# ScalarE copies the turned rows two decays earlier in a scan slot, and makes the two gates behind two decays

## The reference

```
def step(state, inp):                 # selective scan over L = 512 steps
    d, b, c, u = inp
    dA = jnp.exp(d[..., None] * A)
    state = state * dA + (d * u)[..., None] * b[:, None, :]
    y = jnp.einsum('bdn,bn->bd', state, c)
    return (state, y)
...
y = y + D[None, :, None] * x
y = y * silu(z)
...
x = x + scan_part
h = _layernorm(x)
gu_s = h @ shared_gate_up             # shared expert, 2 x 352 = 704 wide
y = routed_experts + _swiglu(gu_s, SI) @ shared_down
out = x + y
```

## Time and profile before

| | |
|---|---|
| time, median of 3 runs (lowest, highest) | 1090.23 us (1086.03, 1094.56) |
| the profiled execution | 1086.13 us, span 1084.4 us |
| busy PE | 911.1 us (84%) |
| busy DVE | 832.5 us (77%) |
| busy POOL | 752.9 us (69%) |
| busy ACT | 514.5 us (47%) |
| granted TensorE clock, mean | 0.908 |

### The profile page before, as it was taken

The page is one execution under the profiler, slowest core; times in us unless marked ns, Lnnn a source line. Parts: engine busy times, 40 slices in busy tenths (PEclk is TensorE's granted clock), DMA queues, the critical chain, the costliest instruction groups (busy, mean ns, idle before and its releaser), DMA issues.

```text
span 1084.4 us, 16598 instructions
## 1 busy us (share of the span) xinstructions
PE 911.1 (84%) x4352; PEld 672.4 (62%) x4353; DVE 832.5 (77%) x1349; ACT 514.5 (47%) x959; POOL 752.9 (69%) x482
## 2 busy tenths in 40 slices
PE   4876656678899888879988899969999899998993
PEld 1322334455566666656656555639999799987992
DVE  4787899999998899988999413869889888988000
ACT  3767634445555454555455222115555455554541
POOL 2544889889898888879895110026888698887872
PEclk9997656789999899999999989989999999999997
DMA  5468921552228322562120230036676767684433
GB/s 169 185 260 306 323 78 59 205 203 77 78 71 308 128 77 65 184 245 80 46 78 29 78 129 10 20 110 192 157 207 185 208 171 200 194 221 102 76 59 38
DMA packets 69987, 152.14 MB, mean 140 GB/s; under 512 B 7585, under 2 KB 23969, under 8 KB 64306
## 3 DMA queue, kind: packets, MB, share of 16 engines
q1 hardware_dynamic: 59410, 126.97, 33.8%
q0 software_dynamic: 10528, 24.65, 11.8%
HBM read 112.80 MB, written 38.80 MB: 140 GB/s over the span
## 4 chain that ended last, share of the span: by engine, by line
PE 49%; DVE 27%; issue 14%; ACT 4%; DMA 2%; POOL 2%; DVEq 1%; SPq 0%; ACTq 0%; POOLq 0%
PE bank L665 10%; PE bank L684 8%; PE bank L769 6%; PE bank L611 6%; PE bank L771 6%; PE bank L770 6%; DVE bank L1342 5%; DVE gs L1356 5%; DVE e_gu_lo L1568 2%; DVE e_gu_hi L1567 2%; DVE bank L1560 2%; DVE p_acc L1286 1%; DVE h_p L1342 1%; PE bank L758 1%; ACT bank L925 1%
## 5 line engine op out<-in xcount | busy, mean ns | idle before, releaser
L1151 POOL TENSOR_TENSOR dbu<-bcs,m_w 128x2048 f32<-128x2048 f32 x64 | 294.0, 4594 | 30.8 <-DVE bank L1342 27.4
L925 ACT ACTIVATE bank<-m_dt,c_a 128x512 f32<-128x512 f32 x256 | 171.3, 685 | 234.2 <-DVE gs L1356 234.2
L1342 DVE TENSOR_TENSOR_SCAN bank<-bank,dbu 128x512 f32<-128x512 f32 x192 | 230.9, 1219 | 15.7 <-ACT bank L925 14.8
L665 PE MATMUL bank<-ws_gu,f_xnT 128*128 128x352 f32 x576 | 202.6, 494 | 30.1 <-ACT f_hT L947 28.3
L611 PE MATMUL bank<-ident,gs 128*128 128x128 f32 x768 | 140.4, 319 | 56.5 <-DVE gs L1356 50.4
L611 PEld LDWEIGHTS bank<-ident,gs 128*128 128x128 f32 x768 | 108.2, 165 | 113.8 <-DVE gs L1356 70.8
L665 PEld LDWEIGHTS bank<-ws_gu,f_xnT 128*128 128x128 f32 x576 | 110.3, 204 | 79.7 <-ACT f_hT L947 29.5
L769 PE MATMUL bank<-e_gu_hi,e_xT_hi 128*128 x376 | 130.1, 346 | 6.1 <-DVEq L1582 3.9
L1356 DVE TENSOR_TENSOR gs<-bank,bcs 128x512 f32<-128x512 f32 x192 | 128.5, 670 | 0.0
L771 PE MATMUL bank<-e_gu_hi,e_xT_lo 128*128 x376 | 122.3, 325 | 0.0
L770 PE MATMUL bank<-e_gu_lo,e_xT_hi 128*128 x376 | 122.1, 325 | 0.0
(11 more groups left out here) (166 smaller groups left out, 1683.7 us busy)
## 6 DMA issues: line engine op xcount, KB each, us to landing
bcs<-bc_scratch SPq DMA_DIRECT2D x32, 1024.0 KB, 9.1
e_gu<-in_wgu SPq DMA_DIRECT2D x16, 1408.0 KB, 9.1
e_dn<-in_wdn SPq DMA_DIRECT2D x16, 512.0 KB
out_rows<-xt SPq DMA_DIRECT2D x18, 256.0 KB, 2.1
p_x<-in_x SPq DMA_DIRECT2D x4, 1024.0 KB, 7.3
u_scratch<-p_u SPq DMA_DIRECT2D x4, 1024.0 KB, 4.0
silu_z_scratch<-p_sz SPq DMA_DIRECT2D x4, 1024.0 KB, 5.0
dt_scratch<-p_dt SPq DMA_DIRECT2D x4, 1024.0 KB, 4.2
```

Source lines behind the costliest of these rows:

```text
L665: last = mm(dst[:, 0:I], lhs[t], ws_gu[:, t, off:off + I], start=t == 0, stop=t == KH - 1)
L925: f(HS[k % RING_H][:], m_dt[:, q % 2, :], ACT.Exp, scale=c_a[:, q, n:n + 1]).then_inc(exp_done, 1)
L1151: g.tensor_tensor(part_, Bs[:, gr * GRP:(gr + 1) * GRP, :], w, ALU.mult).then_inc(dbu_ready, 1)
L1342: v.tensor_tensor_scan(to, h, dbu[:, n, :], 0.0, ALU.mult, ALU.add).then_inc(scan_done, 1)
```

## The change

`GATE_AT` becomes a pair, and HT_AT goes from 4 to 2. ScalarE's two calls of `hT_copy` stand behind the third decay (n = 2, and behind the `skip` of L933 that stands there too) instead of the fifth. The gate of half 0 stays behind the decay n = 9, the gate of half 1 goes behind the decay n = 10. This holds for the 12 slots with rows; the gates also for the last slot of batch 0. No instruction is added or taken away.

```
-GATE_AT, HT_AT, XN_AT, XNT_AT = 9, 4, (14, 10), (15, 15)
+GATE_AT, HT_AT, XN_AT, XNT_AT = (9, 10), 2, (14, 10), (15, 15)
...
-                    if n == GATE_AT:
-                        for c in range(2):
-                            if rows:
-                                gate((j[0] + 1, (q + 1) % TB), c)
-                            elif q == DT - 1:
-                                gate((0, 0), c)
+                    if n in GATE_AT:
+                        c = GATE_AT.index(n)
+                        if rows:
+                            gate((j[0] + 1, (q + 1) % TB), c)
+                        elif q == DT - 1:
+                            gate((0, 0), c)
```

## The result

The changed kernel takes **1102.5 us** (median of 4 runs, 1099.8 to 1104.0) against 1088.4 us of the kernel before (4 runs, 1086.0 to 1094.6): the ratio is 1.0137, with a 95% interval of 1.0098 to 1.0175. It is slower, outside the stated range of 1077 to 1097 us. Its profiled execution has a span of 1098.1 us against 1084.4, 13.7 us more; the busy time of every engine but TensorE (918.6 us against 911.1) is the same within 1.4 us.

What follows compares the result with a forecast made beforehand. It took the slot as a chain closing at VectorE's wait for TensorE at `hidden`; 0 (copies, nine slots), -2.8 (three slots) and 0 (gates) gave about -3 us, 1087 us on the median, range 1077 to 1097.

Steps and rivals of the forecast that it cites:

- What bounds the slot: Whole slot: a chain through several engines, closing where VectorE waits at f_h for TensorE's up product, 19.4 us in twelve slots.
- The copies' own cost: ScalarE's hidden-row copies moved behind `skip`: cost nothing, since the decays behind them could not begin before 547.54 anyway.
- What is late next: TensorE's additions into Y wait for VectorE; of 2.08 us freed, 1.5 only move idle time behind the gate piece.
- the clock term: TensorE's granted clock, nine slots with q above 0: about 0, between 5.1 us of gain and 7 us of loss.
- falls at the same place: Clock case: TensorE's clock falls where it did before; the 0.57 us are not earned, slots alike from the second addition.
- The mixture: Nine slots with q above 0: clock holding, falling at the same place or falling later taken as mixed, sum about 0.
- the falls are tied to no instruction: TensorE's clock: two falls in neighbouring slots are 30.8 us apart, so a changed slot length moves them within the slot.
- Rival (b): Cold stretch settles on additions and pieces behind 552.1 in nearly every slot: +6 to +13 us, 1096 to 1103; chance 0.15.
- The gain a slot, 0.57 us: Slots with q above 0: TensorE's third addition into Y starts at most 0.57 us sooner, passed on to `hidden`.
- The gain of the slots with q = 0: Three slots with q = 0: waits at `hidden` of 0.9 us each bound the gain; 2.8 us taken as earned.
- The gates: ScalarE's gates around decays n = 10 and 11: 0.4 us of wait moves one scan on; value 0, at most 1.2.
- The rule on transposes: Skill rule that transposes do not engage TensorE's full clock: would mean loss in every slot; the forecast held the trace against it.

Runs made afterwards that it cites:

- e3: The changed kernel with unused matrix products filling TensorE's two idle times, ahead of the first addition into Y and behind it, in each slot with rows: 1081.9 us.
- e6: The changed kernel with TensorE's four gate pieces moved forward into its idle times, two of them ahead of the first addition into Y: 1083.1 us.
- e7: The changed kernel with TensorE's gate pieces and also its down pieces moved forward into the idle times: 1073.9 us, ratio 0.9884 to the kernel before.
- e9: The changed kernel with 8 unused products in the first idle time alone, ahead of the first addition into Y: 1083.1 us.
- e8: The changed kernel with the copies behind the decay n = 3, one decay later than in the change: 1086.4 us, ratio 0.9994 to the kernel before.
- e2: The kernel before with the gates alone split over the decays n = 9 and n = 10, copies left behind n = 4: 1084.0 us, ratio 0.9982.
- e10: The kernel before, copies and gates in their old places, with TensorE's gate and down pieces moved forward: 1084.9 us, ratio 0.9977.
- e12: The changed kernel with each slot's first gate piece behind the first addition into Y, so one idle time instead of two: 1096.5 us, ratio 1.0098.

## Why the prediction was wrong

- **What bounds the slot** was read rightly: VectorE at f_h behind TensorE's up product. Nearly all the growth is in that wait, and e3, e6 and e7 shorten the slot through it alone.
- **The copies' own cost**, nothing, held: the decays behind them start when VectorE lets them (394.33), and e3 and e9, with the same copies, are no slower than the kernel before.
- **What is late next** held: `take_y`, then the products of n = 2 and 3 release TensorE, and the idle time moved behind the gate piece (1.96 us, 1.9 foretold). That the 2 us do not reach f_h was right.
- **The step that failed** is the clock term: "I take the three cases as mixed over the nine slots with q above 0, and their sum as about 0". It was worked out with a cold stretch of 3.4 us wherever the clock falls, and with a loss of 0.5 to 1.1 us at most. The runs show falls of 3.5 and of 6.9 us. Where it was 3.5 us (q = 2), the price was the foretold one: the fall came 6.3 to 6.9 us behind `skip`, and the slots took 0.9 to 1.1 us more than before (0.5 and 1.1 were foretold for falls 5.9 and 6.8 us behind it). Where it was 6.9 us the slots took 1.7 to 2.3 us more (q = 1 and 3), in line with the 1.8 to 2.2 of e8. Two of these, with q = 1 in batches 2 and 3, are the forecast's case "falls at the same place": 4.6 and 4.7 us behind `skip`, as in the kernel before (4.4 and 4.7). There the two slots were to be "alike" from the second addition on; they lost 1.7 us each, since the clock did not come back where it did before.
- **The mixture was none.** The clock held in no slot with q above 0. The eight of them that have a next `skip` lost 0.9 to 2.3 us each, 12.9 us together, and the last 2.1 at f_h. The argument behind it, that the falls are tied to no instruction because two of them are 30.8 us apart, does not follow: that is the length of the slot, and falls tied to a place in the slot would show the same. In the change they stayed between 4.6 and 6.9 us behind `skip` and did not wander off the chain. That the same order can have a fall in one slot and none in the next is shown by e8. And the trace of before already had stretches of 10.3 and 6.9 us (from 355.4 and from 485.1 us), which the forecast left out.
- **Rival (b)** put the cold stretch on the chain, and its upper end, 1103 us, is the result; that the number fits is in part luck. It took 12 slots at 1.1 us at most on a base of 1090.2 us; measured were nine at 0.9 to 2.3, a gain in the three with q = 0, some loss behind the slots, and a base of 1088.4. Its chance, 0.15, was too small.
- **The gain a slot, 0.57 us, was too large as well**: with the clock full it was 0.30 us (30.75 to 30.45, in e3 and, without any filling, in two slots of e8), since the chain then closes over the addition of n = 7. The prediction followed the additions to the third and took the rest as work without a pause.
- **The gain of the slots with q = 0** held: they gained 0.33, 0.70 and 1.18 us, 2.2 in all where 2.8 stood. The wait at f_h fell there as foretold, from 0.57, 0.93 and 1.45 us to 0.28 or less in each.
- **The gates**: nothing, as said, and the wait moved one scan on (0.41 to 0.59 us in e2).
- **The rule on transposes** in the Trainium skill (TensorE: Matmul & The Clock Gate, part 4) would by itself have given a loss. The trace does not agree with it: the clock was 1.00 behind 3.50 us of transposes alone. Nor do the runs make transposes the reason: the slots of e8 have the same ones whether the clock stays up or is down for 6.9 us. The filling of e3 was matrix products, so it tells nothing of transposes.
- **The largest omission** was a use for the time: the 2 us that the copies free are worth 11 us once TensorE has pieces to put there (e7 against e10), and cost 14 without them.

## What to carry to other kernels

An engine that is released earlier only starts its first task earlier; list what holds each of its next tasks until the chain that sets the end is reached, and move work into the gap in the same edit. On TensorE count a gap twice, for itself and for the clock behind it, and price a fall at the longest cold stretch that the whole trace shows, not at the one in the slot looked at (here 10.3 us, against 3.5). A few products of no use in the gap tell in one run whether the clock is what costs.

## What the runs showed of the hardware

- In this kernel's slots the granted clock came back behind stretches in which TensorE worked without a pause (3.40 of 3.40 us; 3.30 of 3.30 in the change and in e12), and did not behind those where it worked 2.27 or 1.99 of 3.30 us at half speed: then it was down for 6.9 us instead of 3.5. Work in such a stretch alone doesn't tell the two apart: behind 2.89 of 3.40 us it came back, behind 2.88 of 3.40 it did not, both in e8.
- Filling 1.96 us of idle time with 8 products of 128 columns, 16 records in 1.95 us of TensorE's time in each slot, took 19 to 20 us off the changed kernel (1083.1 us in e9 against 1102.5), and the clock no longer fell in the slots.
- The same order of instructions gave slots of 30.45 us and of 32.3 to 32.7 us in one execution (e8), by the clock alone.
